# The last neighbour sum of a four-layer graph network: rows gathered as three 16-bit terms and summed by node, in place of 32-bit rows summed by column

## The reference, cut to what matters

```python
h = jnp.maximum(_layernorm(x, axis=-1), 0.0)
x = x + _L2_gnn_ref(h, edge_attr_16, edge_index, ...)   # attention, gated by beta
h = jnp.maximum(_layernorm(x, axis=-1), 0.0)
x = x + _L3_gnn_ref(h, src, dst)
# _L3_gnn_ref(mat, row, col):
vals = jnp.take(mat, col, axis=0)
out = jax.ops.segment_sum(vals, row, num_segments=NC)
return out
```

## Time and profile before

| what | value |
|---|---|
| median of 3 runs | 11,695.7 us (11,684.55 to 11,703.09) |
| the profiled execution | 11,690.42 us |
| its span, first to last instruction | 11,688.7 us |
| busy in the span: PE, PEld, DVE, ACT, POOL | 6,256.4, 4,853.4, 6,469.5, 2,647.0, 6,742.7 us |
| beta_phase, from its first DVE operation to the last sum's first | 9,243.28 to 9,326.88 us |
| last sum, first gather to last add | 9,330.30 to 11,671.1 us |
| final_phase, first transpose to the end of the span | 11,671.41 to 11,688.7 us |

### The profile page before, as it was taken

The page is one execution under the profiler, slowest core; times in us unless marked ns, Lnnn a source line. Parts: engine busy times, 40 slices in busy tenths (PEclk is TensorE's granted clock), DMA queues, the critical chain, the costliest instruction groups (busy, mean ns, idle before and its releaser), DMA issues. The chain is left out here.

```text
span 11688.7 us, 111903 instructions
## 1 busy us (share of the span) xinstructions
PE 6256.4 (54%) x29027; PEld 4853.4 (42%) x29027; DVE 6469.5 (55%) x14870; ACT 2647.0 (23%) x8519; POOL 6742.7 (58%) x7099
## 2 busy tenths in 40 slices
PE   8744577777775355555554455555555333333333
PEld 2233455555554333333333455555555333333333
DVE  7799766666664455555554555555555622233223
ACT  0033111111110244444442243444444300000000
POOL 0055566666665566666665455555555466666665
PEclk6555788888887676666666777877777655555555
DMA  0000233333334422222222333333333322222223
GB/s 26 12 10 10 56 76 73 76 76 76 76 75 86 110 46 46 47 47 46 47 46 31 85 85 87 87 87 87 86 87 88 65 46 47 48 47 47 47 47 53
DMA packets 1413627, 706.78 MB, mean 60 GB/s; under 512 B 1170036, under 2 KB 1273944, under 8 KB 1412872
## 3 DMA queue, kind: packets, MB, share of 16 engines
q0 software_dynamic: 254160, 559.07, 19.0%
q1 hardware_dynamic: 1158840, 140.57, 8.6%
HBM read 595.05 MB, written 104.05 MB: 60 GB/s over the span
## 5 line engine op out<-in xcount | busy, mean ns | idle before, releaser
L1042 POOL DMA_INDIRECT l_rows<-h_tab,l_index x1616 | 1525.7, 944 | 942.3 <-issue 452.8
L1425 POOL DMA_INDIRECT l_rows<-h_tab,l_index x1616 | 1527.7, 945 | 868.5 <-issue 472.5
L603 POOL DMA_INDIRECT l_rows<-h_tab,l_words x1616 | 1524.6, 943 | 828.2 <-issue 461.8
L646 PE MATMUL l_sums<-l_onehot,l_rows 128*128 128x128 f32 x3232 | 829.5, 438 | 1599.0 <-issue 875.5
L1560 PE MATMUL l_sums<-l_weighted,l_rows 128*128 128x256 f32 x3232 | 1199.0, 537 | 712.7 <-DVE acc L1487 673.6
L646 PEld LDWEIGHTS l_sums<-l_onehot,l_rows 128*128 128x128 f32 x3232 | 719.6, 328 | 1708.9 <-issue 1076.1
L1947 PE MATMUL l_ps_q<-qtab,h 128*128 x3232 | 831.4, 413 | 1099.6 <-ACT h L1836 783.9
L634 DVE TENSOR_TENSOR acc<-acc,l_sums 128x128 f32 x1616 | 462.6, 286 | 1646.4 <-remote 733.8
L1439 ACT ACTIVATE l_weighted<-l_onehot,l_weights 128x128 f32<-128x128 bf16 x3232 | 987.5, 388 | 1427.2 <-DVE l_onehot L554 1084.1
L1487 DVE TENSOR_TENSOR acc<-acc,l_sums 128x256 f32 x1616 | 677.4, 419 | 1047.8 <-remote 687.4
L759 PE MATMUL src_sums<-tmp 128*128 128x288 f32 x3128 | 1042.2, 486 | 401.8 <-DVE tmp L736 217.7
(11 more groups left out here) (345 smaller groups left out, 11296.6 us busy)
## 6 DMA issues: line engine op xcount, KB each, us to landing
staged<-tmp SPq DMA_DIRECT2D x391, 152.0 KB
l_rows<-h_tab,l_index POOLq DMA_INDIRECT x3232
l_rows<-h_tab,l_words POOLq DMA_INDIRECT x1616
by_src<-words_src SPq DMA_DIRECT2D x96, 152.0 KB
l_kv<-kv_tab,l_words POOLq DMA_INDIRECT x816
l_attr<-in_edge_attr SPq DMA_DIRECT2D x44, 272.0 KB
l_kv<-kv_tab,moments POOLq DMA_INDIRECT x600
h_tab<-h SPq DMA_DIRECT2D x21, 448.0 KB, 3.0
```

Source lines behind the costliest of these rows:

```text
L603: pool.indirect_dma_start(rows[b][:, j, :], None, table, bass.IndirectOffsetOnAxis(ap=words[k % 3][:, at + j, 0:1], axis=0)).then_inc(rows ...
L646: done = nc.tensor.matmul(sums[q % SUMS][:, j, 0:P], rows[b][:, j, :], onehot[b][:, j, :], start=True, stop=True)
L1042: pool.indirect_dma_start(rows[b][:, j, 0:D], None, table, bass.IndirectOffsetOnAxis(ap=index[q // Q16 % WORDS][:, q % Q16 * H + j, :], ax ...
L1425: pool.indirect_dma_start(rows[b][:, j, :], None, h_tab, bass.IndirectOffsetOnAxis(ap=index[q // Q16 % WORDS][:, q % Q16 * H + j, :], axis ...
```

## The change

The table in HBM holds, in place of h (32-bit, 512 bytes a row), three bf16 terms t0, t1, t2 of it: t0 = bf16(h), t1 = bf16(h - t0), t2 = bf16(h - t0 - t1), 768 bytes a row. `beta_phase` makes them in SBUF (two more ACT operations and two more DVE operations per part) and stores them. The last sum gathers rows of three terms, writes its one-hots in bf16, and makes three matmuls per tile into the same bank with the one-hot as stationary operand, so that PSUM receives nodes on partitions. `acc3` is an array of its own, and `final_phase` adds it to x without a transpose. The core of the diff:

```diff
+TERMS = 3
+    terms_tab = nc.dram_tensor("terms_tab", (NB * P, TERMS * D), BF16).ap()
...
# sum_phase
-        rows = [sb(f"rows{b}", [P, H, D]) for b in range(RING)]
-        onehot = [sb(f"onehot{b}", [P, H, P]) for b in range(RING)]
+        rows = [sb(f"rows{b}", [P, H, TERMS * D], BF16) for b in range(RING)]
+        onehot = [sb(f"onehot{b}", [P, H, P], BF16) for b in range(RING)]
...
-                        done = nc.tensor.matmul(sums[q % SUMS][:, j, 0:P], rows[b][:, j, :], onehot[b][:, j, :],
-                                                start=True, stop=True)
+                        for n in range(TERMS):
+                            done = nc.tensor.matmul(sums[q % SUMS][:, j, 0:D], onehot[b][:, j, :], rows[b][:, j, n * D:(n + 1) * D],
+                                                    start=(n == 0), stop=(n == TERMS - 1))
...
# beta_phase, SP
-                norm_store(sp, h_tab, h, h_ready, h_stored)
+                rows = terms_tab.rearrange("(r b p) d -> r p b d", b=LB, p=P)
+                for r in range(R):
+                    sp.wait_ge(split, r + 1)
+                    sp.dma_start(rows[r], terms[r % 2][:].rearrange("p b n d -> p b (n d)")).then_inc(h_stored, 16)
+                sp.wait_ge(h_stored, 16 * R)
...
# beta_phase, ACT
+                def first(r):
+                    act.wait_ge(h_ready, r + 1)
+                    if r >= 2:
+                        act.wait_ge(h_stored, 16 * (r - 1))
+                    nc.scalar.activation(terms[r % 2][:, :, 0, :], h[:, part_of(r), :], ACT.Copy).then_inc(rounded, 1)
+                def second(r):
+                    act.wait_ge(rest_ready, r + 1)
+                    nc.scalar.activation(terms[r % 2][:, :, 1, :], tmp[:, part_of(r), :], ACT.Copy).then_inc(rounded2, 1)
+                for s in range(R + 4):
+                    if s < R:
+                        gate(s)
+                    if 2 <= s < R + 2:
+                        norm_root(nc, act, stat, eps, s - 2, var_ready, root_ready)
+                    if 3 <= s < R + 3:
+                        norm_relu(nc, act, h, tmp, s - 3, centred, h_ready)
+                        first(s - 3)
+                    if s >= 4:
+                        second(s - 4)
...
# beta_phase, DVE
+                def rest(r):
+                    dve.wait_ge(rounded, r + 1)
+                    nc.vector.tensor_tensor(tmp[:, part_of(r), :], h[:, part_of(r), :], terms[r % 2][:, :, 0, :], ALU.subtract).then_inc(rest_ready, 1)
+                def third(r):
+                    dve.wait_ge(rounded2, r + 1)
+                    nc.vector.tensor_tensor(terms[r % 2][:, :, 2, :], tmp[:, part_of(r), :], terms[r % 2][:, :, 1, :], ALU.subtract).then_inc(split, 1)
+                for s in range(R + 5):
+                    if s < R:
+                        attention(s)
+                    if 1 <= s < R + 1:
+                        gate(s - 1)
+                    if 2 <= s < R + 2:
+                        norm_centre(nc, dve, ch, stat, x, tmp, s - 2, root_ready, centred)
+                    if 4 <= s < R + 4:
+                        rest(s - 4)
+                    if s >= 5:
+                        third(s - 5)
...
# final_phase: the tensor block, the two PSUM arrays and the wait on them are gone
-                    nc.vector.tensor_tensor(x[:, here, :], x[:, here, :], turns[r % 2][:, 0:LB, :], ALU.add).then_inc(done, 1)
+                    nc.vector.tensor_tensor(x[:, here, :], x[:, here, :], acc[:, here, :], ALU.add).then_inc(done, 1)
```

More of the change, by code:

```diff
@@ L213, in build @@
             acc = sb("acc1", [P, NB, 2 * D], F32, sums1)
-            acc3 = acc[:].rearrange("p b c -> p (b c)")[:, 0:NB * D].rearrange("p (b c) -> p b c", c=D)
             of = Weights(nc, sums1)
@@ L228, in build @@
                 attend_phase(nc, acc, att, qtab, h, rep, x, skip, ident, place, blk_src, by_src, kv_tab, moments, stat)
-                beta_phase(nc, att, skip, zs, x, h, qtab[:, :, 0:D], moments, stat, eps, of.wz[:], h_tab)
-            sum_phase(nc, "l3", acc3, minus, blk_src, by_src, h_tab)
-            final_phase(nc, acc3, x, ident, out)
+                beta_phase(nc, att, skip, zs, x, h, qtab[:, :, 0:D], moments, stat, eps, of.wz[:], terms_tab)
+        with ExitStack() as last:
+            acc3 = sb("acc3", [P, NB, D], F32, last)
+            sum_phase(nc, "l3", acc3, minus, blk_src, by_src, terms_tab)
+            final_phase(nc, acc3, x, out)
 def rank_phase(nc, x_in, src_in, dst_in, et_in, x, h, tmp, moments, stat, ident, place, minus, before, lane,
@@ L1957, in _, with beta_phase @@
                 sum_up(0, HALVES - 1)
-def beta_phase(nc, acc, skip, zs, x, h, tmp, moments, stat, eps, wz, h_tab):
+def beta_phase(nc, acc, skip, zs, x, h, tmp, moments, stat, eps, wz, terms_tab):
     with ExitStack() as own:
@@ L1973, in beta_phase @@
         att = h
+        terms = [sb(f"terms{n}", [P, LB, TERMS, D], BF16) for n in range(2)]
+        rounded, rest_ready, rounded2, split = sem("rounded"), sem("rest_ready"), sem("rounded2"), sem("split")
         with nc.Block() as block:
@@ L1989, in gate @@
                     nc.scalar.activation(z[:, 1, part_of(r)], z[:, 0, part_of(r)], ACT.Exp).then_inc(e_ready, 1)
-                for r in range(R):
-                    gate(r)
+                def first(r):
+                    act.wait_ge(h_ready, r + 1)
                     if r >= 2:
[L1993 to L1999, removed]
+                        act.wait_ge(h_stored, 16 * (r - 1))
[13 more added lines that the diff above has]
+                        second(s - 4)
             @block.vector
@@ L2027, in _, with final_phase @@
                 ch.link(nc.vector.reciprocal(rden[:], rden[:]))
[L2028 to L2039, removed]
+                def rest(r):
[15 more added lines that the diff above has]
+                        third(s - 5)
+def final_phase(nc, acc, x, out):
     R = NB // LB
@@ L2044, in final_phase @@
         sem = lambda name: own.enter_context(nc.semaphore(name))
-        turns = [own.enter_context(nc.psum_tensor(f"last_turn{s}", [P, LB + 1, P], F32)) for s in range(2)]
-        turned, done, stored = sem("last_turned"), sem("last_sum"), sem("out_stored")
+        done, stored = sem("last_sum"), sem("out_stored")
         with nc.Block() as block:
[L2048 to L2055, removed]
             @block.vector
@@ L2060, in _ @@
                     here = part_of(r)
-                    dve.wait_ge(turned, r + 1)
-                    nc.vector.tensor_tensor(x[:, here, :], x[:, here, :], turns[r % 2][:, 0:LB, :], ALU.add).then_inc(done, 1)
+                    nc.vector.tensor_tensor(x[:, here, :], x[:, here, :], acc[:, here, :], ALU.add).then_inc(done, 1)
             @block.sync
```

## The result

The changed kernel took 11,764.92 us (median of 5 runs, 11,742.11 to 11,771.37), the kernel before 11,695.7 us. The ratio is 1.0049, with a 95% interval of 1.0035 to 1.0063, which is 41 to 74 us. The forecast was 11,760.

What follows compares the result with a forecast made beforehand. In the last sum POOL's gathers, plus stops from held-back PE completions, were taken as the bound. 39 + 11 + 15 - 2 = +63 on the profiled 11,690.4 us gave 11,760 for a run; own range 11,725 to 11,830, 8-in-10 range 11,700 to 11,885.

Steps and rivals of the forecast that it cites:

- POOL's chain in the last sum: Last sum: POOL's 1,616 gathers, 0.943 us each and 0.30 us apart, make 2,009 of the stage's 2,341 us.
- held-back completions: Last sum: while POOL gathers unbroken, PE's completions drain about one per gather; the ring fills, POOL stops; 0.213 us per gather.
- Three matmuls per tile, +39 us: Last sum: PE instructions per gather go from 4 to 6, POOL's stops from 0.213 to 0.237 us per gather; +39 us.
- Rows of 768 bytes, +11 us: Last sum: wider rows lengthen each of POOL's 1,616 gathers by 7 ns; +11 us, ends 0 and +45.
- Padding tiles, 0: End of the last sum: padding reads, taken as set by number of rows, add 0; at most 35 us more.
- beta_phase, +15 us: beta_phase: DVE's added work, longer ACT-DVE hand-overs and a bigger last store; `h_stored` waits already met; +15 us, ends 8 and 20.
- final_phase, -2 us: final_phase: without transposes, seven adds of 1.12 us follow a start of about 0.5 us; -2 us, ends -3 and 0.
- The sum: Whole kernel: 39 + 11 + 15 - 2 = +63 us, giving 11,760 us for a run; forecast's chance 0.60.
- A: Rival, last sum: bf16 completions are never held back, POOL's stops vanish, 342 us less; 11,378 us; chance 0.13.
- C: Rival, last sum: stops grow in proportion to PE instructions or the whole backlog builds; +139 to +172, 11,860 to 11,895 us; chance 0.13.
- B: Rival, last sum: PE's instruction count doesn't matter, or three matmuls share one weight load; +24, 11,720 us; chance 0.14.
- "Slower" with 0.74: Whole kernel: chance 0.74 of measuring slower, against 0.12 same (11,672 to 11,719 us) and 0.14 faster.

Runs made afterwards that it cites:

- f32_by_node: Kernel before, still 32-bit, but one-hot as held operand and rows moving, so sums stand by node without final transposes; ratio 1.0006 to the kernel before.
- six_buffers: Changed kernel with six buffers for the terms in beta_phase instead of two; beta_phase 99.1 us, ratio 1.0026 to the kernel before.
- six_matmuls: Changed kernel with six 16-bit matmuls per tile in the last sum, each term twice; last sum 2,387.8 us, ratio 1.0092 to the kernel before.

## Why the prediction was right, and where it was not

- **POOL's chain in the last sum, and held-back completions as the cause of its stops.** Right on the chip of the forecast: the same waits, stops of 0.217 us per gather, PE's instructions one by one. On four other chips the cause is absent, the last sum is 2,037 us, and the forecast's largest term is nothing.
- **Three matmuls per tile, +39 us.** The direction was right, the term was mis-sized. The three stages of the earlier trace rows, from which 0.024 us for two instructions was read, differ in more than the count. With matmuls alone added, 6 to 12 instructions cost 0.0275 us. The pauses, for which the term stood, grew by 15.7 us in the pair of chip A and by 10 us from f32_by_node to six_buffers, and the medians of chip B leave 3 us for the whole last sum. POOL's commonest run between stops went from 24 gathers to 20, not to 16. PE's time for a quad, 1.44 us, was rightly taken as hidden; its matmuls start 0.107 us apart, which agrees with the 320 ns a tile of the prediction.
- **Rows of 768 bytes, +11 us.** Measured up to 5 us. The 951 ns of the earlier trace rows that it was taken from belong to another stage; beside unchanged stages of one trace the gathers moved by 2 to 3 ns.
- **Padding tiles, 0.** From the issue of the last gather to the last add it is 13.7 us before and 13.8 after, so no extra time piled up there.
- **beta_phase, +15 us.** The work was right: without the store wait it is 15.5 us. The step that failed is "ACT's waits on `h_stored` are met by the store of two parts before, some 20 us old": measured, the store was issued 3.6 us before ACT went on, ACT stood 34.7 us, and the stage grew by 30.9.
- **final_phase, -2 us.** -1.8 in the changed kernel and in f32_by_node.
- **The sum.** +63 was forecast, +51 stands in the traces, and 41 to 74 is what the runs give. That it fits is luck: two terms that were too large by 27 us together stand against one that was too small by 16. On chip C the same change costs 30 us, nearly all of it in beta_phase.
- **The rivals.** A (16-bit completions are not held back) is wrong: where 32-bit ones are, they are too. C is refuted by six_matmuls; B is refuted between 6 and 12 instructions and not told from the forecast's mechanism between 4 and 6. "Slower" with 0.74 rested on the gathers and was borne out mostly by beta_phase.
- **Slips in the working.** The add of the earlier trace rows at 9,828.96 belongs to the quad that PE began at 9,814.70, not to the one of 9,819.68, so these sums came later still than the prediction says. 951 less 943 ns is 8, not 7. And the ends named for the terms, with +39 kept, give 11,740 to 11,800 us, or 11,835 with the padding's 35, where 11,725 to 11,830 is written.

No kernel of these beats the one before measurably. f32_by_node, which has the sums by node without the terms, is at 1.0006 (0.9996 to 1.0015): the 2 us that it saves at the end are below what can be told.

What stays open: whether the number of PE's instructions or the time that they occupy PE sets how late the news of them comes (that PE is still at work on the awaited quad is excluded), what a deeper ring would bring on a chip with stops (the stops there come to some 300 us in all), and what makes a chip hold completions back, for good or for a time.

## What to carry to other kernels

Where a double buffer is freed by a store, write down the step at which the store is issued and the step at which the buffer is wanted again; "two parts before" says nothing if the part takes five steps to finish. When an engine is hidden, halving its work brings nothing, and the work moved ahead of the loop to enable it is paid in full. Before a wait that no instruction explains is priced, look at the same kernel on a second chip. And before two traces are subtracted, see where each lies among the runs of its kernel.

## What the runs showed that was not expected

- One and the same program takes 11,553 to 11,696 us on two chips and 9,929 to 9,935 us on four others. In the changed kernel's traces of both kinds the single instructions of the last sum last the same (gathers 948 and 946 ns, matmuls 308). The difference is in when DVE and POOL see PE's sums while POOL issues indirect DMAs back to back: 9 us after the matmul in the median, against 0.4.
- Where they are late, the price per gather grows with the number of PE instructions, but more slowly than the number: 1.414, 1.430, 1.442, 1.470 us at 2, 4, 6, 12 in one trace each.
- A gather of 128 rows takes POOL 943 to 948 ns for rows of 256, 512 or 768 bytes.
- In six_matmuls the granted clock of the stretch was 0.61, with PE busy for 928 of the 2,000 us. In the other three it was 0.50 (the 1.2 GHz level), with PE busy for 208 to 718 us.
